# Attention on one core: value products of two blocks issued together, a ring of exponentials twice as long, a new order of rounds, and late allocation of four weight tensors

## The reference

```
qkv = x @ w_qkv                        # 16 heads of 16 channels
attn = softmax(q @ k^T * SCALE)        # per head, 512 x 512
x1 = layernorm(x + attn @ v @ w_proj + b_proj)
top 2 of 8 experts by x1 @ Wg.T, capacity 1.25, gates = softmax of the two logits
y = x1 + sum over the two of gate * (gelu(a) * g) @ W2[e],  [a, g] = x1 @ W1[e]
out = layernorm(y)
```

## Time and profile before

| what | value |
|---|---|
| median of 3 runs | 3407.72 us (3406.1 to 3410.54) |
| profiled execution, its own time | 3412.06 us |
| its span | 3410.2 us |
| TensorE busy | 3043.8 us (89%) |
| VectorE busy | 2537.0 us (74%) |
| ScalarE busy | 2217.3 us (65%) |
| GpSimd busy | 1618.4 us (47%) |

### The profile page before, as it was taken

How to read it: one execution, slowest core, us unless ns; L and a number is a source line. 1 busy time by engine, 2 the same in 40 slices (tenths; PEclk the granted TensorE clock), 3 DMA queues, 4 the chain that set the end, 5 groups by cost and what they waited for, 6 DMA issues and landing times. The chain is left out here.

```text
span 3410.2 us, 63298 instructions
## 1 busy us (share of the span) xinstructions
PE 3043.8 (89%) x21035; PEld 1947.2 (57%) x21035; DVE 2537.0 (74%) x5828; ACT 2217.3 (65%) x4280; POOL 1618.4 (47%) x1412
## 2 busy tenths in 40 slices
PE   4999999999999999999999949999999999999640
PEld 3444444444444444445444338878878888888640
DVE  3888888888888888888888556666666666666459
ACT  2888878788887878787887625555555555555420
POOL 5455656565656556565656123333333333333223
PEclk7999999999999999999999869999999999999875
DMA  2455555433333333333333147667667766776549
GB/s 89 145 164 172 162 163 171 119 99 80 104 81 99 88 97 88 94 96 83 102 79 94 45 112 154 141 141 155 141 139 155 149 142 145 151 145 141 123 141 316
DMA packets 412527, 435.22 MB, mean 128 GB/s; under 512 B 223016, under 2 KB 313520, under 8 KB 412208
## 3 DMA queue, kind: packets, MB, share of 16 engines
q1 hardware_dynamic: 356432, 346.76, 39.8%
q0 software_dynamic: 51168, 67.68, 9.5%
q10 hardware_dynamic: 4608, 16.78, 1.2%
HBM read 183.93 MB, written 146.15 MB: 97 GB/s over the span
## 5 line engine op out<-in xcount | busy, mean ns | idle before, releaser
L1020 DVE TENSOR_REDUCE peak<-ps 128x1 f32<-128x512 f32 x2048 | 1337.5, 682 | 293.0 <-PE ps L701 292.3
L799 ACT ACTIVATE probs<-ps 128x512 f32<-128x512 f32 x2048 | 1124.3, 611 | 174.8 <-PE ps L711 165.6
L1288 POOL DMA_INDIRECT x<-out,token x270 | 444.5, 1646 | 856.9 <-ACT out L1363 747.9
L1302 PE MATMUL ps_hid<-x_hi,stack 128*128 128x512 f32 (+1 forms) x2304 | 707.8, 391 | 131.5 <-DVE hid L1417 101.4
L711 PE MATMUL ps<-stack 50*128 50x512 f32 x2048 | 785.2, 453 | 3.5 <-DVE peak L1020 2.9
L701 PE MATMUL ps<-stack 48*128 48x512 f32 x2048 | 753.0, 445 | 19.6 <-DMA stack<-qk_lo 13.6
L701 PEld LDWEIGHTS ps<-stack 48*128 48x128 f32 x2048 | 336.5, 188 | 465.9 <-issue 220.2
L1302 PEld LDWEIGHTS ps_hid<-x_hi,stack 128*128 128x128 f32 x2304 | 428.1, 195 | 238.4 <-issue 156.3
L727 PE MATMUL ps_pv<-probs,v 128*17 128x512 f32 x4096 | 545.8, 605 | 1.2 <-ACT probs L799 1.2
L551 POOL DMA_INDIRECT expert_rows<-row,slot x256 | 254.8, 995 | 410.1 <-DVE token L1000 325.8
L1302 PE MATMUL ps_hid<-x_lo,stack 128*128 128x512 f32 (+1 forms) x1152 | 446.9, 388 | 0.0
(11 more groups left out here) (176 smaller groups left out, 4404.9 us busy)
## 6 DMA issues: line engine op xcount, KB each, us to landing
probs<-in_L_ffn_W SPq DMA_DIRECT2D x288, 256.0 KB, 5.0
stack<-qk_hi SPq DMA_DIRECT2D x1024, 64.0 KB, 2.2
expert_rows<-blank SPq DMA_DIRECT2D x81, 520.0 KB, 3.9
probs<-in_L_ffn_W SPq DMA_DIRECT2D x72, 512.0 KB, 7.6
stack<-qk_lo SPq DMA_DIRECT2D x512, 64.0 KB, 2.2
quarters<-expert_rows SPq DMA_DIRECT2D x252, 128.0 KB
xs<-in_L_attn_x SPq DMA_DIRECT2D x32, 512.0 KB, 4.3
x<-row SPq DMA_DIRECT2D x32, 512.0 KB, 3.3
```

The lines of the kernel that those rows point to most:

```text
L799: act.activation(probs[:, j % RING, :], ps[it.bank(("cols", s * UNITS + j))][:], ACT.Exp, scale=SCALE).then_inc(s_exp, 1)
L1020: dve.tensor_reduce(peak[s % 2][:, u:u + 1], ps[it.bank(("rows", n))][:], AX.X, ALU.max, negate=True).then_inc(s_max, 1)
L1288: pool.indirect_dma_start(x1_dram, bass.IndirectOffsetOnAxis(ap=token[n % 2][:, t:t + 1], axis=0), out[n % 2][:, t, :], None, bounds_check ...
L1302: last = pe.matmul(ps_hid[f % 2][:, part, 0:cols(n)], w[n % 2][k][:, w_cols], xx[n % 2][:, k, 0:cols(n)], start=i == 0, stop=i == 3 * KT - 1)
```

## The change

1. `ORDER` is written anew. The step "pv2" issues the value products of the block before and of this block, one behind the other. It stands in the eight even blocks; the odd ones have none. 
2. Rounds move with it: peak3 from c1 to the end of c2, peak1 from c10 to the start of c9, logitT from c4 to c5, turn2 from c6 to c5, turn3 ahead of pairs 1 to 3 of c10 and next to place; xT and qk2 stand one pair earlier or in the same place, proj1 one pair later.
3. `RING` is 16 tiles, four blocks of exponentials, and ScalarE's wait asks for the value product of four blocks earlier.
4. `w2_buf` is gone from the outer allocation; `experts` allocates w2_hi and w2_lo (two each) itself.

```
-RING = 8
+RING = HG * TILES
...
-    [0, 1, "xT", 2, "pv", 3],
-    [0, "x1T", 1, "pv", "peak3", 2, 3],
-    ["logit", 0, 1, "turn1", 2, 3, "pv"],
-    [0, 1, "qk0", 2, 3, "pv"],
-    [0, 1, "qk1", 2, 3, "logitT", "pv"],
-    [0, 1, "peak0", 2, 3, "pv"],
-    [0, 1, 2, "pv", "turn2", 3],
-    [0, "qk2", 1, 2, 3, "pv"],
-    [0, 1, "qk3", 2, 3, "pv"],
-    [0, 1, "v0", 2, 3, "pv"],
-    [0, "place", "peak1", 1, 2, "turn3", 3, "pv"],
-    [0, 1, "oT", 2, "pv", 3],
-    [0, 1, "proj0", 2, "pv", 3],
-    [0, 1, "proj1", 2, 3, "pv"],
-    ["peak2", 0, "turn0", 1, 2, 3, "pv"],
-    [0, 1, "v1", 2, 3, "pv"],
+    [0, "xT", 1, 2, "pv2", 3],
+    [0, "x1T", 1, 2, 3],
+    ["logit", 0, 1, "turn1", 2, 3, "peak3", "pv2"],
+    [0, 1, "qk0", 2, 3],
+    [0, 1, "qk1", 2, 3, "pv2"],
+    [0, 1, "peak0", 2, 3, "logitT", "turn2"],
+    [0, 1, 2, "pv2", 3],
+    [0, "qk2", 1, 2, 3],
+    [0, 1, "qk3", 2, 3, "pv2"],
+    ["peak1", 0, 1, "v0", 2, 3],
+    [0, "place", "turn3", 1, 2, 3, "pv2"],
+    [0, 1, "oT", 2, 3],
+    [0, 1, "proj0", 2, 3, "pv2"],
+    [0, 1, 2, "proj1", 3],
+    ["peak2", 0, "turn0", 1, 2, 3, "pv2"],
+    [0, 1, "v1", 2, 3],
...
+        elif step_ == "pv2":
+            STEPS += [("values", c_ - 1, "pv"), ("values", c_, "pv")]
...
-                            wait(act, s_pv, (b + off) * 16 + (4 * g + j // HG - 1))
+                            wait(act, s_pv, (b + off) * 16 + (4 * g + j // HG - 3))
...
-        w1_hi, w1_lo, w2_hi, w2_lo = weights.w1_hi, weights.w1_lo, weights.w2_hi, weights.w2_lo
+        w1_hi, w1_lo = weights.w1_hi, weights.w1_lo
+        w2_hi = [sb(f"w2_hi{i}", [P, FT, DIM], F32R)[:] for i in range(2)]
+        w2_lo = [sb(f"w2_lo{i}", [P, FT, DIM], F32R)[:] for i in range(2)]
...
-        w2_buf = ctx.enter_context(nc.sbuf_tensor("w2_buf", [P, 4, FT * DIM], F32R))
```

More of the change, by code:

```diff
@@ L80 @@
             STEPS.append(("pair", c_ // TILES, HG * (c_ % TILES) + step_))
+        elif step_ == "pv2":
+            STEPS += [("values", c_ - 1, "pv"), ("values", c_, "pv")]
         else:
-            STEPS.append(("values" if step_ == "pv" else "round", c_, step_))
+            STEPS.append(("round", c_, step_))
 NAMES = [step_[2] for step_ in STEPS if step_[0] == "round"]
@@ L208, with __init__ @@
 class Weights:
-    def __init__(self, stacks, w2_buf, probs, w1, w2, s_raw1, s_raw2):
+    def __init__(self, stacks, probs, w1, w2, s_raw1, s_raw2):
         self.s_raw1, self.s_raw2 = s_raw1, s_raw2
@@ L216, in __init__ @@
         self.w1_hi, self.w1_lo = [[flat[i + j:i + j + KT] for j in (0, 2 * KT)] for i in (0, KT)]
-        self.w2_hi, self.w2_lo = [[w2_buf[:, 2 * j + i].rearrange("p (k d) -> p k d", k=FT)
-                                   for j in range(2)] for i in range(2)]
         raw = probs[:].rearrange("p r n -> p (r n)")
@@ L1579, in transformer_layer @@
         stacks = [ctx.enter_context(nc.sbuf_tensor(f"stack{i}", [P, PAIRS, SEQ], F32R)) for i in range(2 * GROUPS)]
-        w2_buf = ctx.enter_context(nc.sbuf_tensor("w2_buf", [P, 4, FT * DIM], F32R))
         probs = ctx.enter_context(nc.sbuf_tensor("probs", [P, RING, SEQ], F32))
-        weights = Weights(stacks, w2_buf, probs, w1, w2,
+        weights = Weights(stacks, probs, w1, w2,
                           ctx.enter_context(nc.semaphore("s_raw1")), ctx.enter_context(nc.semaphore("s_raw2")))
```

## The result

The changed kernel takes 3467.94 us (3463.53 to 3470.95, 4 runs), against 3409.13 us of the kernel before in the same runs: ratio 1.0169, 95% interval 1.0150 to 1.0188. It is slower, as forecast, but by 59 us where 16 were forecast, and it lies 6 us above the top of the range. The profiled execution has a span of 3465.6 us.

What follows compares the result with a forecast made beforehand. Bound by VectorE's stretches and GpSimd's chain, with TensorE waiting on both. Pieces of +0.2, +1.3 and -0.95 make +0.6 us a period, +18 over 31 iterations; 3408 + 18 less 2 gives 3424 us, range 3362 to 3462.

Steps and rivals of the forecast that it cites:

- qk0 to c5: Period piece from the qk0 round to block c5: 0.2 us longer, 7.18 for 6.95.
- c5 to c9: Period piece from block c5 to c9, bound by VectorE's work: 1.3 us longer, 15.65 for 14.34.
- c9 to token: Period piece from block c9 to token in c12: 0.95 us shorter, two value products instead of three.
- token to qk0: Period piece from token to qk0: unchanged at GpSimd's chain of 25.0 us; TensorE's own way about 24.8.
- Switches and the second product: TensorE in each iteration: fewer switches, second product 0.87 us; own work of 53 to 54 falls by 1.3 to 2.3.
- Gaps that run VectorE dry: Behind the double products of c4, c8 and c0: VectorE idles 1.3 to 1.5 us.
- Count and row_count: Routing steps on VectorE: still meet GpSimd's qk addition; missing it is worth up to 1.5 us an iteration.
- Ring, late weights, peak3: Ring of 16 and late weight allocation: nothing; the later peak3's DMA just fits before c4's cols.
- Rival 1: TensorE's saving of 40 to 71 us arrives whole or in part: 3337 to 3400 us, 33%.
- Rivals 2 and 3: 2: peak3's DMA delays c4's cols, 3455 us, 13%; 3: gaps and saved switches cancel, 3408 us, 12%.
- the ends of attention: Where products wait for exponentials at attention's ends: may give back 2 us of the total.

Runs made afterwards that it cites:

- light_after: The changed kernel with VectorE's reductions and ScalarE's exponentials halved: 3297.63 us; the kernel before with the same halving: 3314.91 us.
- pairs_only: The kernel before with value products in twos at the even blocks' old places, other rounds unmoved: 3521.66 us, ratio 1.0312 to the kernel before.
- ring_only: The kernel before, old order and single products, with only the ring of 16, its wait and the late weights new: 3406.96 us, ratio 0.9980.
- rounds_only: The changed kernel's new order, but with a single value product for each block: 3459.45 us, ratio 1.0128 to the kernel before.

## Why the prediction was right in direction and wrong in size

By its own steps, for the pieces of one period (us):

| piece | before | forecast | measured |
|---|---|---|---|
| qk0 to c5 | 6.95 | 7.18 | 7.19 (1023.23 to 1030.42) |
| c5 to c9 | 14.34 | 15.65 | 16.83 (1030.42 to 1047.25), 15.69 without a fall |
| c9 to token | 12.2 | 11.3 | 11.37 (1047.25 to 1058.62) |
| token to qk0 | 25.0 | 25.0 | 25.4 (997.82 to 1023.23) |
| period | 58.5 | 59.1 | 60.8, in a third 59.7 |

- **Switches and the second product.** The second product is right: 0.86, 0.87 forecast. That TensorE's own work falls by 1.3 to 2.3 us is not borne out. With both readers light the period fell by 0.34 only, and light_after takes 55.46 us with no wait of any weight in its steady periods, where 53 to 54 less the saving would be 51 to 53. The sum rested on that term only through the 24.8 us below.
- **Gaps that run VectorE dry.** Right in place; in size near it at c0 (1.31) and c8 (1.88, in a period with a fall), too large at c4 (0.95), against 1.3 to 1.5 forecast. A fourth one, 0.96 at c12, was not forecast. On the old places the pairs bring the loss (pairs_only against ring_only). On the new places they don't: the 1.3 us that I gave to c5 to c9 came out (15.69 measured, 15.65 forecast; its own terms add up to 15.70), but rounds_only has 15.82 there with single products. So that the double gap causes it is not shown. And ScalarE is fed through the same banks: halving VectorE's work alone doesn't turn the sign.
- **c5 to c9: the step that failed.** I priced the piece at TensorE's full clock throughout. I let TensorE wait for VectorE's banks there, and put what follows from the wait at nothing. Measured: the pause of 1.07 us takes the clock to half, qk3 takes 2.2 us (1041.60 to 1043.81, the start of the next pair) instead of 1.4, the products 2.2 instead of 1.84. That is the 1.15 us between 15.69 and 16.83. Over the run it is 22 of the 43 us that were missing.
- **Token to qk0: the second step that failed.** I took GpSimd's 25.0 us as the bound and TensorE's way as 24.8, just inside it. Measured: 25.4, and the waits for GpSimd are gone, that for x_t_lo too, whose staying I had named as a sign of being right. TensorE and its readers bound the stretch now; which of them is not separated. pairs_only has 25.8 there and rounds_only 25.2, so pairs and places both add to it. Over 31 periods it is 12 us more. The other 9 us are 2 us that I took off for the ends of attention, 2 us from c9 to the token (11.37 for 11.3), and a rest that was not taken apart.
- **Count and row_count.** Right that they meet GpSimd again (1.04 and 0.92 us). Moving them away is worth 1.0% in the kernel before. In the changed kernel it is 1.1%, but with the falls of the clock in it.
- **Ring, late weights, peak3.** Nothing, as forecast: ring_only is 0.2% under before, and no wait of L711 for the peak's DMA shows up in the steady periods.
- **Rival 1** didn't come, and even with VectorE and ScalarE light only 0.34 us of it can be seen. Rivals 2 and 3 didn't come. That the moved rounds alone cost 1.3% was not among the rivals.

The direction was right in part by luck. The forecast called it a longer period by VectorE's gaps, and put 0.92 of its 1.3 us in c5 to c9 on moved rounds. At full clock the period got longer by 1.15 us instead of 0.6, and rounds_only gets longer by more without any double gap.

## What to carry to other kernels

When operations without output for the other engines are put together to save switches, compare the longest gap with the work that the buffers let those engines hold, and do so for each reader, not only the busiest. Time the moved rounds alone as well: here they cost 1.3% of the kernel by themselves. A pause of TensorE costs more than its length where the clock falls behind it: a wait that grows towards 1 us, as here, is to be priced twice, with the full clock and with half of it. Two small VectorE steps took 0.92 and 1.04 us here instead of 0.16 while GpSimd worked on qk's results; moving them by two pairs won 1.0%, where the change lost 1.7%.

## What was unexpected of the hardware

A single pause of 1.07 us in an otherwise busy stretch is followed by a clock of 0.5 (matmuls of 0.40 us taking 0.69) in two periods of three, while pauses of 0.42 us in the same place, one in each period of the kernel before, never brought it down. Four useless matmuls in the pause took all of these falls away but one and made the kernel 0.66% faster. That two whole-array value products follow each other at the pure stream distance (0.86 against 0.98) was expected from the estimate, and is now measured.
